# Selective scan on one core: units of two channel tiles against units of four

## The reference, cut to what matters

```python
def step(h, inp):
    dt_t, u_t, B_t, C_t = inp
    A_bar = jnp.exp(dt_t[..., None] * A)
    h = A_bar * h + dt_t[..., None] * B_t[:, None, :] * u_t[..., None]
    y = jnp.sum(h * C_t[:, None, :], axis=-1)
    return (h, y)
...
y = y + u * D
y = y * _silu(z)
```

## Time and profile before

| | us |
|---|---|
| median of 3 runs | 3904.94 (3896.28 to 3906.43) |
| the profiled execution | 3901.24 |
| its span, first to last instruction | 3899.0 |
| mean granted clock of TensorE, share of full | 0.948 |
| busy in the span: PE, DVE, ACT, POOL | 3383.3, 2821.2, 2321.3, 959.3 |
| scan stage in the span | about 258 to 992 |

### The profile page before, as it was taken

One profiled execution on the slowest core, in us unless ns is written; L12 is line 12 of the kernel. 1 busy time (PEld: TensorE's weight loads), 2 busy tenths in 40 slices (PEclk: granted clock), 3 DMA queues, 4 the chain that ended last, 5 costly groups with the idle time before them and its releaser, 6 DMA issues. The chain is left out here.

```text
span 3899.0 us, 57139 instructions
## 1 busy us (share of the span) xinstructions
PE 3383.3 (87%) x18410; PEld 1677.7 (43%) x18410; DVE 2821.2 (72%) x4083; ACT 2321.3 (60%) x4496; POOL 959.3 (25%) x914
## 2 busy tenths in 40 slices
PE   7857888888689897989686999999999999995896
PEld 3325666666455554767431222222222222223664
DVE  6638999999355554545468888888888888853665
ACT  5758999999110000222124888888888888882342
POOL 7548888888000000000121000000000000001100
PEclk9979999999899998999887999999999999997998
DMA  3458765671211102020221000000000010001101
GB/s 130 159 148 187 151 143 144 146 147 49 94 40 47 30 31 60 1 67 11 86 83 34 14 21 13 20 19 19 22 13 20 13 24 14 13 4 58 33 22 43
DMA packets 205143, 231.50 MB, mean 59 GB/s; under 512 B 67987, under 2 KB 135187, under 8 KB 204117
## 3 DMA queue, kind: packets, MB, share of 16 engines
q1 hardware_dynamic: 204900, 228.35, 22.4%
HBM read 160.93 MB, written 67.37 MB: 59 GB/s over the span
## 5 line engine op out<-in xcount | busy, mean ns | idle before, releaser
L1687 DVE TENSOR_REDUCE attn_part_max<-attn_pM 128x1 f32<-128x1024 f32 x1024 | 1204.1, 1219 | 161.9 <-PE attn_pM L1742 158.7
L1667 ACT ACTIVATE attn_probs<-attn_pE 128x512 f32<-128x512 f32 x2048 | 1089.8, 597 | 205.1 <-PE attn_pE L1791 201.1
L1791 PE MATMUL attn_pE<-attn_q,attn_k_exp 128*128 128x512 bf16 x2048 | 628.2, 385 | 31.1 <-ACT attn_q L1639 24.7
L542 POOL TENSOR_TENSOR scan_dbu<-scan_du,scan_b_all 128x2048 f32<-128x2048 f32 x128 | 579.9, 4540 | 74.2 <-DVE scan_h L604 70.4
L1762 PE MATMUL attn_pA<-attn_probs,attn_v 128*32 128x512 f32 x4096 | 560.3, 604 | 0.0
L556 ACT ACTIVATE scan_hcT<-scan_hT,scan_c_t 128x256 f32<-128x256 f32 x1024 | 523.8, 664 | 0.0
L604 DVE TENSOR_TENSOR_SCAN scan_h<-scan_abar,scan_h,scan_dbu 128x512 f32<-128x512 f32 x384 | 487.2, 1280 | 30.8 <-POOL scan_dbu L542 12.0
L571 ACT ACTIVATE scan_abar<-scan_delta,scan_decay 128x512 f32<-128x512 f32 x512 | 450.5, 880 | 23.7 <-DVE scan_h L604 23.7
L619 PE MATMUL scan_hT<-scan_ident,scan_h 128*128 128x128 f32 x2048 | 368.7, 287 | 89.2 <-ACT scan_hcT L556 66.7
L1791 PEld LDWEIGHTS attn_pE<-attn_q,attn_k_exp 128*128 128x128 bf16 x2048 | 139.0, 97 | 607.0 <-ACT attn_probs L1667 457.8
L956 PE MATMUL moe_pP<-moe_w_qkv,moe_xT 128*128 128x384 f32 x1024 | 354.2, 507 | 10.7 <-DVE moe_acc L846 10.7
(11 more groups left out here) (273 smaller groups left out, 3848.8 us busy)
## 6 DMA issues: line engine op xcount, KB each, us to landing
scan_b_all<-mid_BC SPq DMA_DIRECT2D x64, 1024.0 KB, 10.4
attn_q<-mid_q_parts SPq DMA_DIRECT2D x224, 64.0 KB, 2.4
mid_gT<-front_gT SPq DMA_DIRECT2D x8, 1024.0 KB, 8.0
mid_uT<-front_uT SPq DMA_DIRECT2D x8, 1024.0 KB, 9.4
mid_dT<-front_dT SPq DMA_DIRECT2D x8, 1024.0 KB, 4.3
scan_delta<-mid_dT SPq DMA_DIRECT2D x16, 512.0 KB, 3.8
scan_u_in<-mid_uT SPq DMA_DIRECT2D x16, 512.0 KB, 4.9
scan_g<-mid_gT SPq DMA_DIRECT2D x16, 512.0 KB, 3.8
```

What stands on the lines that cost most here:

```text
L542: nc.gpsimd.tensor_tensor(dbu[:, p % NDBU, :, :, :], du_pair, b_pair, ALU.mult).then_inc(dbu_ready, 1)
L1667: nc.scalar.activation(probs[:, kt % 4, h, :], pE[:, bank(item), :], ACT.Exp, scale=SCALE).then_inc(exp_done, 1)
L1687: nc.vector.reduce_max(part_max[:, h, j, i:i + 1], pM[:, m % 2, :], AXIS_X).then_inc(max_read, 1)
L1791: nc.tensor.matmul(pE[:, bank(item), :], k_exp[:, par, kt * 128:(kt + 1) * 128], q[:, qc, h, :], start=True, stop=True).then_inc(e_psum, 1)
```

## The change

A unit becomes one chunk with all four channel tiles: 2 sequences x 4 chunks = 8 units, still 16 states each. `G` now runs to 128; `k` still to 512. The turned states are handled by time tile (`i`, 512 of them): for one tile of 128 steps the four channel tiles lie side by side, so that one copy is 128x512. `h` shrinks from all states to a ring of three `G`, so the last column must be kept elsewhere: DVE writes `states[:, n, 0:4]` with `reduce_max` over one element (128x4 out of 128x4, `keep_state`), and the next chunk's scan starts from there. B is loaded once per chunk instead of once per chunk and pair. The gates' first loads move behind `c_psum`, since the rows of C now use their buffer. DVE's `finish` has four operations per unit and comes after k = 9 of the next unit. PE no longer turns a channel tile as soon as its own scan is done, but a time tile when all four scans of a `G` are done.

```diff
-    MP = 2
-    UNITS = B * (NDI // MP) * CPB
+    UNITS = B * CPB
-    K_UNIT = NS * MP
-    NDBU, NHC = 3, 3
+    K_UNIT = NS * NDI
+    I_UNIT = NS * TPC
+    NDBU, NH, NHC = 3, 3, 8
-    D_AT = (6, 10)
-    FINAL_AT = 4
+    D_AT = (4, 6, 8, 10)
+    LAG, HOLD, FINAL_AT = 6, 7, 9
+        states = s.sb("states", [128, NS, NDI])
-        dbu = s.sb("dbu", [128, NDBU, 2, MP, CH])
-        h = s.sb("h", [128, NS, MP, CH])
-        hcT = s.sb("hcT", [128, NHC, TPC, MP * 128])
-        y_acc = s.ps("y_acc", [128, MP, CH])
-        hT = s.ps("hT", [128, 4, CH])
+        dbu = s.sb("dbu", [128, NDBU, NDI, CH])
+        h = s.sb("h", [128, NH, NDI, CH])
+        hcT = s.sb("hcT", [128, NHC, NDI * 128])
+        y_acc = s.ps("y_acc", [128, NDI, CH])
+        hT = s.ps("hT", [128, 2, CH])
...
                 load_unit(1)
-                load_gate(0)
                 for i in range(4):
                     load_b(1, i)
+                sp.wait_ge(c_psum, 1)
+                load_gate(0)
                 load_gate(1)
...
-                        at_least(pool, scan_done, (p - NDBU + 1) * 2 * MP)
+                        at_least(pool, scan_done, (G - NDBU + 1) * NDI)
+                        b_row = b_all[:, u % 2, n, :].unsqueeze(1).broadcast_to([128, NDI, CH])
+                        nc.gpsimd.tensor_tensor(dbu[:, G % NDBU, :, :], du[:, u % 2, :, :], b_row, ALU.mult).then_inc(dbu_ready, 1)
+                        if n == NS // 2 and u + 1 < UNITS:
                             make_du(u + 1)
...
+                def evacuate(i):
+                    G, tile = divmod(i, TPC)
                     u, n = divmod(G, G_UNIT)
+                    act.wait_ge(turned, i + 1)
+                    at_least(act, sum_done, i - NHC + 1)
+                    nc.scalar.activation(hcT[:, i % NHC, :], hT[:, i % 2, :], ACT.Copy, scale=c_t[:, u * TPC + tile, n:n + 1]).then_inc(hc_ready, 1)
...
-                    if G >= 2:
-                        evacuate(G - 2, m)
+                    if k >= LAG:
+                        evacuate(k - LAG)
...
+                def keep_state(G):
+                    dve.wait_ge(scan_done, (G + 1) * NDI)
+                    nc.vector.reduce_max(states[:, G % NS, :], h[:, G % NH, :, CH - 1:CH], AXIS_X).then_inc(state_kept, 1)
...
                     dve.wait_ge(abar_ready, k + 1)
+                    if m == 0:
+                        dve.wait_ge(dbu_ready, G + 1)
+                        at_least(dve, turned, (G - NH + 1) * TPC)
+                        at_least(dve, state_kept, G - NH + 1)
+                    if u % CPB:
+                        dve.wait_ge(state_kept, G - NS + 1)
+                    state = states[:, n, m:m + 1] if u % CPB else 0.0
+                    nc.vector.tensor_tensor_scan(h[:, G % NH, m, :], abar[:, k % 2, :], dbu[:, G % NDBU, m, :], state, ALU.mult, ALU.add).then_inc(scan_done, 1)
+                    if m == 0 and G:
+                        keep_state(G - 1)
+                    if u and k % K_UNIT == FINAL_AT:
                         finish(u - 1)
...
+                def turn(i):
+                    G, tile = divmod(i, TPC)
+                    pe.wait_ge(scan_done, (G + 1) * NDI)
+                    at_least(pe, hc_ready, i - 1)
+                    for m in range(NDI):
+                        last = nc.tensor.transpose(hT[:, i % 2, m * 128:(m + 1) * 128], h[:, G % NH, m, tile * 128:(tile + 1) * 128], ident[:])
                     last.then_inc(turned, 1)
...
+                    turn(i)
+                    ready = u * I_UNIT if u and i % I_UNIT < HOLD else i - 1
+                    for _ in range(2):
+                        if added < ready:
+                            add(added)
+                            added += 1
+                    if tile == TPC - 1 and n in D_AT:
                         skip(u, D_AT.index(n))
```

More of the change, by code:

```diff
@@ L482, in part @@
                 def part(view, u):
[L483 to L484 removed]
+                    return view[:, :, u * CH:(u + 1) * CH]
                 def load_unit(u):
@@ L570, in _ @@
                     at_least(act, scan_done, k - 1)
-                    nc.scalar.activation(abar[:, k % 2, :], delta[:, u % 2, m, :], ACT.Exp, scale=decay[:, mp * MP + m, n:n + 1]).then_inc(abar_ready, 1)
+                    nc.scalar.activation(abar[:, k % 2, :], delta[:, u % 2, m, :], ACT.Exp, scale=decay[:, m, n:n + 1]).then_inc(abar_ready, 1)
                     if k == 1:
@@ L575, in _ @@
                         act.wait_ge(c_psum, 1)
-                        nc.scalar.activation(c_t[:].rearrange("p t n -> p (t n)"), hT[:, 3, :], ACT.Copy).then_inc(c_ready, 1)
+                        nc.scalar.activation(c_t[:].rearrange("p t n -> p (t n)"), hT[:, 1, :], ACT.Copy).then_inc(c_ready, 1)
                         act.wait_ge(c_ready, 1)
-                    if G >= 2:
-                        evacuate(G - 2, m)
-                for G in (LAST - 2, LAST - 1):
-                    for half in range(2):
-                        evacuate(G, half)
+                    if k >= LAG:
+                        evacuate(k - LAG)
+                for i in range(LAST * TPC - LAG, LAST * TPC):
+                    evacuate(i)
             @block.vector
@@ L641, in _ @@
                 for t in range(NT):
-                    last = nc.tensor.transpose(hT[:, 3, t * NS:(t + 1) * NS], c_rows[:, t * 128:(t + 1) * 128], ident[0:NS, 0:NS])
+                    last = nc.tensor.transpose(hT[:, 1, t * NS:(t + 1) * NS], c_rows[:, t * 128:(t + 1) * 128], ident[0:NS, 0:NS])
                 last.then_inc(c_psum, 1)
-                for k in range(LAST * MP):
-                    G, m = divmod(k, MP)
+                added = 0
+                for i in range(LAST * TPC):
+                    G, tile = divmod(i, TPC)
                     u, n = divmod(G, G_UNIT)
-                    if k == MP:
+                    if i == 1:
                         pe.wait_ge(c_ready, 1)
-                    turn(k)
-                    if m == 0 and G >= 2:
-                        add(G - 2, 1)
-                    if m == 1 and G >= 1:
-                        add(G - 1, 0)
-                    if m == 1 and n in D_AT:
+                    turn(i)
[5 more added lines that the diff above has]
+                    if tile == TPC - 1 and n in D_AT:
                         skip(u, D_AT.index(n))
-                add(LAST - 2, 1)
-                add(LAST - 1, 0)
-                add(LAST - 1, 1)
+                for i in range(added, LAST * TPC):
+                    add(i)
         s.clear()
```

96 lines of the change are left out of this document (27 added, 69 removed).

## The result

The changed kernel takes **3835.53 us** (median of 4 runs, 3835.25 to 3836.50) against 3905.68 (median of 4, 3896.28 to 3906.97) for the kernel before on the same chip: ratio **0.9826 [0.9809, 0.9843]**, 70 us less. The forecast was 3830, in 3812 to 3862. The profiled execution took 3835.25 us, with a span of 3833.4, against a span of 3899.0 before. All that follows compares these two spans, 65.6 us apart, and "after" is the changed kernel.

A forecast was written before the change was run, and what follows sets the result against it. ACT was taken to set the scan's pace at 1.34 us per k, DVE close behind. Stretch -80, start +3.0 and tail with store +3.3 summed to -74: 3830 us against the median, range 3812 to 3862.

The forecast's parts named there:

- ACT set the pace, by its copies' fixed cost: Scan stage: ACT paces at 1.34 us per k; 512-wide copies step 0.57 instead of 0.71 for two, making ACT 1.19.
- DVE 1.20 per k, the maximum 0.08: Scan stage: four scans of 1.18 us plus a new maximum of 0.08 make 4.80 per G, 1.20 per k on DVE.
- Rival 2: Scan stage: DVE held 0.3 us at each maximum, or equal engines lose as much handing over: +28, 3858 us; chance 0.15.
- Balanced: Main case for the scan stage: ACT at 1.19 and DVE at 1.20 us per k nearly equal, 3830 us; chance 0.75.
- Stretch -80: From first to last scan: 631 us against 710.6, so -80.
- Start +3.0: Before the first scan: delta and u of unit 0 are twice the bytes, 1.5 us each, so B comes 3.0 later.
- Tail +1.8: Last scan to store of y: turn, four copies, last add and four finishes take 6.2 us instead of 4.4.
- The stop of 12 us: Early scan stage: DVE's 12.0 us wait for POOL, as u's loads stood behind broadcasts of B, would go.
- POOL and DMA at nothing: Scan stage: POOL's 76.3 us a unit fits under 79; halving B's loads is worth nothing in the even part.
- PE at nothing: Scan stage: PE's transposes take 0.88 of 1.20 us per k and its catch-up fits; uncovered, 1 us a unit.
- Rival 4: Scan stage: PE at the lower clock needs 1.76 us per k; at 40% of the stage 3946 us; chance 0.03.
- The rest of the program at nothing: Five stages behind the scan: no term in the sum, a difference of 0.

The follow-up runs named there:

- Experiment 1: Changed kernel with each copy of a turned tile split back into two of 256 columns: 3896.43 us, beside 3899.35 for the kernel before.
- experiments 6 and 7: Changed kernel with the last columns kept by a VectorE copy (4254.77 us), or by an elementwise maximum of the column with itself (4254.15 us), instead of reduce_max.
- the repeats: Both kernels unchanged, timed and profiled a second time: the kernel before 3894.57 us, the changed kernel 3828.52 us.
- experiment 2: Kernel before with B broadcast for the first two units alone, 8 of its 64 loads: 3889.44 us, beside 3901.26 for the kernel before.

## Why the prediction was right, point by point

- **ACT set the pace, by its copies' fixed cost: right and shown.** The copy's step was forecast as 0.57 from the widths of another stage and is 0.57; ACT per k 1.19, and 1.188 where ACT sets the pace. Experiment 1 gives the time back when only this is undone. The second price given, 613 ns by the Trainium skill, *ScalarE: Activation LUTs*, What ACT_TABLE_LOAD costs, is too high for this copy from PSUM; the exp, whose source is in SBUF, does have it (0.613, median of its steps). One reading was wrong without effect: "busy time near 300" is 372.5, since 728 ns is the copy's length and neighbours overlap; the sum went by steps.
- **DVE 1.20 per k, the maximum 0.08: the right mechanism, a little too dear.** It adds some 0.05 to a G, which is 4.77 instead of 4.80, a unit 78.6 to 78.8 instead of 79.2. Rival 2 (held at each maximum) falls: the scan starts at 440.50, 0.05 behind the maximum's start and ahead of its end at 440.60. So the rule cited from the Trainium skill, *VectorE: DVE Perf Modes*, The DRAIN you can't avoid, does not hold for these neighbours as the prediction read it; it left out that section's own exception, that a next operation that is not held starts earlier, and that is what these rows show. But a small operation isn't cheap for its size, as experiments 6 and 7 show. The forecast asked what a *small* operation costs; that the earlier trace rows is a reduction too, the kind that doesn't wait, was not part of its argument, and that part of its success is luck.
- **"Balanced": right, closer than thought.** Where DVE sets the pace a k takes 4.765 / 4 = 1.191, where ACT does 1.188; so removing the maxima gives only 1 to 2.5 us.
- **Stretch -80: -81.0** (-80.1 between the repeats). Misses cancel: the units with start values, but for unit 2, are 0.4 to 0.6 shorter each, some 3 us, and of the 1.4 for PE at the lower clock DVE's waits show 0.25; the wait for `c_t` is 3.04 instead of 0.6 (0.6 to 2.6 in the eight other profiles with the same start), and unit 2 lost 0.9 to PE.
- **Start +3.0: +3.7.** `du` starts 2.8 later, as forecast (266.07 against 263.27), but B, behind twice the bytes, lands 3.8 later, not 3.0. This row moves from trace to trace: in the ten profiles that have the changed kernel's loads the first scan starts at 275.1 to 277.3, in the three with the old scan at 273.1 to 274.0, so 3.0 is as near as 3.7.
- **Tail +1.8: +2.9.** The failed step is "four copies at 4 x 0.57 + 0.1". They come every 0.87, each waiting for PE, which turns, adds and turns through two `hT` buffers; a copy's step in the steady part isn't its step in a chain. The store's +1.5 was 1.4.
- **The stop of 12 us: right and shown** by experiment 2 (8.6 to 11 us). The forecast took the whole of it from one trace; in the second it is smaller.
- **POOL and DMA at nothing: right in this profile.** From 290 to 905 us DVE waits for ACT alone, 0.7 us in all. But in unit 0 POOL has no lead, and in five later runs DVE waited 0.8 to 2.1 for it there.
- **PE at nothing: nearly.** The failed words are "no idle time of PE longer than a finish remains": true, and beside the point, as the clock fell where PE was at work half the time. Rival 4's mechanism is there, for 3.4 or 6.8 us in each of four units instead of a quarter of the stage, and costs 0.9.
- **The rest of the program at nothing: wrong by +7.4.** The stages behind the scan have the same code and took 2906.5 before, 2914.0 after. In repeats it was 2902.5 and 2911.5; in all the kernels with the changed scan 2906.0 to 2919.5, median 2911.2 of 11, and in the three with the old scan 2902.5 to 2906.5. Of the 7.4, 4.8 lie in the causal attention (363.6 to 368.4), most of it at one place, PE's first matmuls behind its loop's branch. The timeline of PE there, before and after:

```profile
1712.46 0.48 PE L1173 MATMUL causal_pS<-causal_kT,causal_qT 64*128 64x128 f32 x2 [1.95 <-issue]
1714.33 0.70 PE L1173 MATMUL causal_pS<-causal_kT,causal_qT 64*128 64x256 f32 x2 [1.39 <-ACT causal_probs L1162]
```

```profile
1644.13 0.79 PE L1163 MATMUL causal_pS<-causal_kT,causal_qT 64*128 64x128 f32 x2 [5.52 <-issue]
1646.32 1.22 PE L1163 MATMUL causal_pS<-causal_kT,causal_qT 64*128 64x256 f32 x2 [1.40 <-ACT causal_probs L1152]
```

PE stands 5.52 us instead of 1.95, waiting for nothing that the profile shows, and its next matmuls take 1.22 us where they took 0.70; the granted clock in the 8 us from there is 0.50, before 0.68. In all 11 profiles with the changed scan this wait is 4.3 to 5.7 us; in the three with the old one it is 2.0 once and absent twice. So the wait goes with the program, not with the run. That the place of the code among the engine's instructions does this is a guess that wasn't tried, and the rest of the 7.4 is open.

In sum the scan's own part was forecast as -74 and is -73.0; the forecast of 3830 is 5.5 below the median of the first comparison, mostly for the five stages behind. It is only 1.5 above that of the second, 3828.52, but there the kernel before took 3897.79 and not the 3904.94 from which the forecast started: the change was forecast as 75 us and measured as 70 and 69, and the closer hit is luck.

## What to carry to other kernels

When one engine's work is many operations of equal kind, take the fixed part of one from the steps between neighbours at two widths, and ask at once what stands just beneath it: here widening the copies brought ACT from 1.34 to 1.19 us a k, where DVE at 1.19 ends the gain. A wait that only one trace shows can be smaller in the next (the stop, 11 and 8.6 us), so differences of a few us want a second trace of both kernels. A small VectorE operation beside a busy GpSimd is to be chosen by its ports, not its size: as a reduction it cost 0.05 us, as a copy or a two-input operation 3.5. And a stage that is made more even can still leave TensorE half empty where sums are held back; in some units the granted clock fell there, so look at it and not only at idle pieces.

## What the runs showed of the hardware that was not expected

- A 128x4 copy, and a 128x4 maximum of two SBUF inputs, on VectorE last 3.54 and 3.53 us beside GpSimd's products of 4.53, ending with them; a 128x4 reduction lasts 0.15. The scan, with one SBUF tensor, one PSUM tensor and a start value in SBUF, doesn't wait.
- TensorE's granted clock fell to 0.50 for 3.4 or 6.8 us around a stretch in which it worked 0.63 of each 1.19 us, in units 1 to 4 of one profile and 4 to 7 of another of the same kernel, and eight matmuls then took 1.94 instead of 1.04 us. Units with the same stretch and no fall are in both.
- The first matmul behind one loop branch of PE waited 4.3 to 5.7 us in 11 kernels and 0 to 2.0 in three profiles of two others, with the same code at that place.
